# A two-layer graph network on one core: the leaky slope of the attention weights is split between ScalarE and VectorE

## The reference, cut to what matters

```python
scores = leaky_relu(e_s[edge_src] + e_d[edge_dst], 0.2)
m = segment_max(scores, edge_dst)
ex = exp(scores - m[edge_dst])
denom = segment_sum(ex, edge_dst)
msg = (ex / denom[edge_dst])[:, :, None] * h[edge_src]
agg = segment_sum(msg, edge_dst)
```

## Time and profile before

| | us |
|---|---|
| median of 3 runs | 2749.72 |
| lowest and highest of them | 2741.72, 2752.97 |
| the profiled execution, its own time | 2740.57 |
| span of its trace | 2738.8 |
| busy: PE, VectorE (DVE), GpSimd (POOL), ScalarE (ACT) | 1679.5, 1652.3, 1444.6, 833.9 |
| mean granted TensorE clock, share of full speed | 0.802 |

### The profile page before, as it was taken

The page is one execution under the profiler, slowest core; times in us unless marked ns, Lnnn a source line. Parts: engine busy times, 40 slices in busy tenths (PEclk is TensorE's granted clock), DMA queues, the critical chain, the costliest instruction groups (busy, mean ns, idle before and its releaser), DMA issues. The chain is left out here.

```text
span 2738.8 us, 38544 instructions
## 1 busy us (share of the span) xinstructions
PE 1679.5 (61%) x9983; PEld 1342.2 (49%) x9983; DVE 1652.3 (60%) x2687; ACT 833.9 (30%) x2134; POOL 1444.6 (53%) x1557
## 2 busy tenths in 40 slices
PE   4367534677655544486655777504477767767688
PEld 4255423455543433486544566403355545545577
DVE  6455763677654545676424655796366657668675
ACT  3144210000000000465212222205355545534454
POOL 3655676655656664526155555477665655530050
PEclk8599857788876776588777999856689888878899
DMA  4535544555423333344152545454555555331010
GB/s 137 183 101 159 178 140 123 170 174 157 120 81 92 95 92 106 112 142 131 51 175 81 163 154 160 161 190 128 157 166 170 172 164 158 106 101 32 4 43 31
DMA packets 132988, 346.47 MB, mean 127 GB/s; under 512 B 39881, under 2 KB 66521, under 8 KB 119347
## 3 DMA queue, kind: packets, MB, share of 16 engines
q0 software_dynamic: 66144, 180.94, 23.5%
q1 hardware_dynamic: 63407, 158.51, 16.5%
q10 hardware_dynamic: 3364, 6.16, 0.7%
HBM read 262.24 MB, written 83.28 MB: 126 GB/s over the span
## 5 line engine op out<-in xcount | busy, mean ns | idle before, releaser
L1366 PE MATMUL ms_ps_m<-ms_msg,ms_pick 128*128 128x260 f32 x1408 | 415.6, 458 | 287.1 <-issue 199.8
L892 POOL DMA_INDIRECT e_ring<-table,e_index x465 | 442.6, 952 | 252.2 <-issue 137.6
L1347 DVE TENSOR_TENSOR ms_msg<-e_ring,ms_ps_w 128x1040 f32<-128x1040 f32 (+1 forms) x352 | 436.6, 1240 | 141.8 <-issue 128.0
L1366 PEld LDWEIGHTS ms_ps_m<-ms_msg,ms_pick 128*128 128x128 f32 x1408 | 313.0, 229 | 389.7 <-issue 332.2
L1366 PE MATMUL ms_ps_m<-ms_msg,all_xn 128*128 128x272 f32 x1408 | 386.0, 437 | 191.5 <-issue 167.1
L892 POOL DMA_INDIRECT e_ring<-table,l_index x369 | 353.9, 959 | 227.3 <-issue 111.1
L1366 PEld LDWEIGHTS ms_ps_m<-ms_msg,all_xn 128*128 128x128 f32 x1408 | 290.0, 212 | 287.3 <-issue 218.9
L767 PE MATMUL sc_ps_e<-sc_keys,sc_hot 125*128 125x100 bf16 (+1 forms) x3840 | 322.7, 241 | 168.6 <-DVE all_xn L712 141.7
L767 PEld LDWEIGHTS sc_ps_e<-sc_keys,sc_hot 125*128 125x128 bf16 x3840 | 276.8, 104 | 238.8 <-issue 123.4
L934 POOL DMA_INDIRECT w_staged<-table,l_stage_index x256 | 257.3, 1005 | 183.5 <-issue 66.9
L670 ACT ACTIVATE sc_rows<-sc_ps_b 125x512 bf16<-125x512 f32 x320 | 171.2, 598 | 433.6 <-PE sc_ps_b L755 251.8
(11 more groups left out here) (513 smaller groups left out, 2743.3 us busy)
## 6 DMA issues: line engine op xcount, KB each, us to landing
ahead<-w_staged SPq DMA_DIRECT2D x32, 1056.0 KB
e_ring<-ahead SPq DMA_DIRECT2D x32, 1056.0 KB
ahead<-e_ring SPq DMA_DIRECT2D x20, 1040.0 KB
e_ring<-ahead SPq DMA_DIRECT2D x20, 1040.0 KB
e_ring<-table,e_index POOLq DMA_INDIRECT x465
all_acc<-ahead SPq DMA_DIRECT2D x27, 256.0 KB
ahead<-all_acc SPq DMA_DIRECT2D x27, 256.0 KB
e_ring<-table,l_index POOLq DMA_INDIRECT x369
```

The source lines that it names most:

```text
L892: pool.indirect_dma_start(out=g.ring[:, slot * QUAD + i // GT, i % GT, :], out_offset=None, in_=s.table[:, :], in_offset=bass.IndirectOffs ...
L1347: dve.tensor_tensor(msg[:, b, :, 0:R].rearrange("p t (h o) -> p t h o", h=H), ring[:, bass.ds(slot, 1), :, :].rearrange("p a t (h o) -> p ...
L1366: mm = pe.matmul(ps_m[b][:, 0:W], pick[:, b, t, :], msg[:, b, t, :], start=t == 0, stop=t == GT - 1)
```

## The change

Nothing is altered outside of `edge_weights`. The four PSUM banks `ps_t` become one tensor, of which two pairs of banks serve as two buffers of 640 columns, `lean`. For each line ScalarE writes 0.2 times the line into a `lean` buffer (function `slopes`), and VectorE takes the maximum of the line and the copy (`raise_line`). ScalarE writes copy i when all additions of the part have been made and VectorE has used copy i-2; VectorE waits for copy i on the new semaphore `leaned`. PE now waits, before it turns anything back, for the last maximum of the last part, since it writes into the same banks.

```diff
-        ps_t = [m.ps(f"ps_t{i}", [P, 4 * P]) for i in range(4)]
+        ps_all = m.ps("ps_t", [P, 4, 4 * P])
+        ps_t = [ps_all[:, i, :] for i in range(4)]
+        lean = ps_all.rearrange("p (a i) c -> p a (i c)", a=2)[:, :, 0:CL]
...
+        by_head, leaned = m.sem("by_head"), m.sem("leaned")
+        adds = GH * (2 if self_loops else 1)
+        lines_of = lambda part: [line[:, h, :] for line in (full, src_line) for h in range(part * GH, (part + 1) * GH)]
+        added = lambda part: H + part * (adds + 3 * GH) + adds
...
             pe.wait_ge(copied, banks)
+            pe.wait_ge(by_head, added(groups - 1) + 2 * GH)
...
+            def slopes(part):
+                for i, line in enumerate(lines_of(part)):
+                    act.wait_ge(by_head, added(part) + max(i - 1, 0))
+                    act.activation(lean[:, i % 2, :], line, ACT.Copy, scale=NEG).then_inc(leaned, 1)
+
+            for part in range(groups):
+                slopes(part)
+
             def exponentials(part):
...
-                for line in (full, src_line):
-                    add_each(heads, lambda h: dve.scalar_tensor_tensor(out=line[:, h, :], in0=line[:, h, :], scalar=NEG, in1=line[:, h, :], op0=ALU.mult, op1=ALU.max))
+                lines = lines_of(part)
+                for first in range(0, 2 * GH, GH):
+                    def raise_line(i):
+                        dve.wait_ge(leaned, part * 2 * GH + i + 1)
+                        return dve.tensor_tensor(lines[i], lines[i], lean[:, i % 2, :], ALU.max)
+                    add_each(range(first, first + GH), raise_line)
```

More of the change, by code:

```diff
@@ L1015, in edge_weights @@
         shifted, exp_ready, back_turned, back_copied = *(m.sem(n) for n in ("shifted", "exp_ready", "back_turned")), between.back_copied
-        by_head = m.sem("by_head")
+        by_head, leaned = m.sem("by_head"), m.sem("leaned")
+        adds = GH * (2 if self_loops else 1)
+        lines_of = lambda part: [line[:, h, :] for line in (full, src_line) for h in range(part * GH, (part + 1) * GH)]
+        added = lambda part: H + part * (adds + 3 * GH) + adds
         banks = H * CT // 4
@@ L1148, in _ @@
                     add_each(heads, lambda h: dve.scalar_tensor_tensor(out=full[:, h, :], in0=dst[:, h, :], scalar=2.0, in1=full[:, h, :], op0=ALU.mult, op1=ALU.max))
-                for line in (full, src_line):
-                    add_each(heads, lambda h: dve.scalar_tensor_tensor(out=line[:, h, :], in0=line[:, h, :], scalar=NEG, in1=line[:, h, :], op0=ALU.mult, op1=ALU.max))
+                assert heads_done[0] == added(part)
+                lines = lines_of(part)
[4 more added lines that the diff above has]
+                    add_each(range(first, first + GH), raise_line)
                 add_each(heads, lambda h: dve.tensor_tensor(src_line[:, h, :], src_line[:, h, :], full[:, h, :], ALU.subtract))
```

## The result

| | before | changed |
|---|---|---|
| median of 3 runs, us | 2749.72 | 2780.83 |
| lowest and highest, us | 2741.72, 2752.97 | 2763.69, 2799.22 |
| span of the profiled execution, us | 2738.8 | 2797.5 |
| ratio of the times, with its 95% interval | | 1.0115 [1.006, 1.0171] |

A forecast was written before the change was run, and what follows sets the result against it. VectorE was taken to bound the weights stages, but the message stage's start and POOL's restart to count. Delays of 0.5 (first layer) and 6.2 us (second) sum to +6.7, from median 2749.7 to 2756.5 us; range 2745 to 2773.

The forecast's parts named there:

- Price of the copy and of the maximum: Weights stages, per 640-column line: ScalarE's copy to PSUM 0.715 us, VectorE's maximum against PSUM 0.82 us.
- Price of a part: Weights stages: eight lines handed from ScalarE to VectorE cost each part 1.7 us more, 0.87 us a line against 0.745.
- Table load: ScalarE, after the last slope copy: 1.3 us in the second layer, hidden at no cost in the first.
- Order of ScalarE's work: Second layer: all exponentials and copies back follow the last slope copy, ending at 1893.9, so messages start 14.6 us late.
- ten copies 10.24: Second layer, ScalarE: part 0's ten copies back take 10.24 us, from 1871.4 to 1881.6.
- Ten more copies 10.0: Second layer, ScalarE: the ten copies back after part 1's exponentials take 10.0 us, from 1883.9 to 1893.9.
- those 9 us: Second message stage: 9 us between the second step's sum and POOL's restart, by which a start can be late unharmed.
- How much of the late start reaches the end: Message stages: 0.5 of 1.7 us in the first layer, 6.2 of 14.6 in the second; partial shift, chance 0.55.
- the whole late start comes through: Rival, both message stages: the full 1.7 + 14.6 = 16.3 us reaches the end, 2766 us; chance 0.27.
- the late start is hidden altogether: Rival, second message stage: gathers and their transfers pace it, so 0 to +2 us, 2751; chance 0.13.
- POOL runs freer: Rival, weights stages: gathers beside the maxima no longer slowed, 2.5 us gained, 2747 us if POOL bounds; chance 0.05.

The follow-up runs named there:

- free conditions: Conditions of the last five runs: the kernel before took 2317.16 us, then 2311.89, where it had taken 2739 to 2756 in the conditions of the result.
- the order alone: Kernel before, no slope copies, but both parts' exponentials behind the last subtraction: 2798.3 us, ratio 1.0129; in the free conditions 2309.79 us, 0.9989.
- banks of their own: Changed kernel with four other PSUM banks for slope copies, part 1's made after part 0's exponentials and ten copies back: 2777.83 us, ratio 1.0054.
- the pause: The order alone, with some 9 us of ScalarE idle time between the tenth copy back and the second exponentials: one run, 2774.65 us.
- the kernel with extra instructions: Kernel before, with 60 tiny memsets on VectorE behind the second layer's last subtraction: one run, 2731.22 us for 2739.31 of the kernel before.
- POOL was held: POOL waits before its third message-stage quad for all copies back: the order alone so held (second layer only) 2755.63 us, ratio 1.0055; changed kernel 2780.14, 1.0073.
- the changed kernel held: Changed kernel, with POOL waiting for all copies back before its third quad of message-stage gathers: 2780.14 us, ratio 1.0073.

## Why the prediction was wrong

**Price of the copy and of the maximum: right.** 0.707 us for the 0.715 of the sum, and 0.82 for 0.82.

**Price of a part: right in size.** 1.4 to 1.9 us for 1.7; a line took 0.83 us in a steady row for the 0.87 forecast.

**Table load: right.** 1.30 us in the second layer, hidden in the first, where it ran at 377.57 and the exponentials waited 2.65 us more for the subtractions. The Trainium skill ("ScalarE: Activation LUTs", What ACT_TABLE_LOAD costs) would have 2.66 us; no row here shows the drain of 1.38 that it adds.

**Order of ScalarE's work: right; its pace: wrong.** From the end of the last slope copy to the last copy back the prediction had 27.4 us (1866.5 to 1893.9). In the free conditions it is 27.3 (from 1519.1 to 1546.4). **In the conditions of the result it is 55.6** (from 1880.7 to 1936.3). This is the step that failed: "ten copies 10.24" was priced at the pace of the earlier trace rows, and these ten took 38.6 us, because TensorE's updates of `back_turned` came up to 28 us late and ScalarE waited for them. "Ten more copies 10.0" was right. In the first layer the five copies had gaps of 1.22 and 2.35 us in the same way, and its 1.7 us became 5.4.

The sign of it stood in the rows. The earlier trace rows have a hold that ends with "remote", 9 us after the sum that should have ended it, and the prediction booked those 9 us as slack that a late start could use up. They were a late update. Had it been read so, the same lateness could have been asked of the row of copies. Why the ten copies of part 0 ran without a gap before, beside gathers into the ring as well, was not found.

**How much of the late start reaches the end: not refuted.** The prediction let 8.4 of 14.6 us pass, because POOL's restart lay 9 us later than the sum that frees it. In the changed kernel it came 8.1 us after the first message (1949.58 to 1957.67) for 17.1 before, and 8.7 was forecast. Whether the end followed is less clear. The change's own profile has the message stage at 557.6 us for 556.2, so all of its late start came through; the order alone, banks of their own and the pause have 544.4, 548.9 and 551.6. But the kernel with extra instructions, which started the stage 4 us late, has 545.2, so this length scatters by as much as is asked for. The times do not settle it either: the change lost 31 us for 42.5 + 5.4 of late start, the order alone 35.5 by its ratio and 42.6 by the medians for 43.2. Where POOL was held, nearly all came through or more: 15 us for 18.0, and 20 for 14.5 in the changed kernel held. By the prediction's own steps with the 28.3 us put in, the sum is 6.7 + 28.3 = 35 us, or 2784.7, for 2780.8 measured.

**The rivals.** That the whole late start comes through gives 16.3 us and 2766 without the gaps, and 2794 with them; that lies above the median, though within the three runs. That the late start is hidden altogether is false for the result and true in the free conditions: with a first message that waits 29.6 us for its transfer, 11 us more of tail cost nothing. That POOL runs freer may hold there, and for more than its 2.5 us: 8 to 9 us between the medians (0.9962). The Trainium skill ("SBUF — State Buffer", Who interferes with whom) has that VectorE with two SBUF inputs contends with a GpSimd instruction that reads SBUF, and with one it does not. The trace agrees (up to 1.16 us for 0.95, and no long block beside the maxima against PSUM), but it also has a block that outlasts twelve VectorE instructions, which a lock for one instruction does not give. That the change's gain in the free conditions comes from the missing blocks is read from the profiles; the order alone, which keeps VectorE's slope, has 0.9989 [0.997, 1.0008] and no block in its profile. The change and the order alone have nearly the same median (2309.22 and 2309.79); what differs more is the kernel before in their two batches (2317.16 and 2311.89). So the timed runs do not settle it.

**What stays open.** What makes TensorE's updates and the other engines' register instructions late, and whether the two have one cause. The same kernel on the same chip took 2739 us in one batch of runs and 2317 in the next, eight minutes later, and 2312 on another chip. The late updates go with POOL's gathers (tail 23.8 us for 51.8 when held, 30.7 for 55.8), and a pause of ScalarE does not help. How much of the 427 us between the conditions they make was not tried. The Trainium skill ("Runtime: NRT & Kernel Launch", Instruction fetch mechanics) has that each sequencer refills its instructions by a DMA queue of its own and that this is mostly hidden. The trace agrees in so far as it lists such packets, none longer than 1.7 us in the changed kernel's first profile and none in its gaps, so late refills are not what opened them. Nor was it tried whether fewer gathers in this stretch, with the rest made up later, would help.

## What to carry to other kernels

Before work is moved, look at what the receiving engine already does between its pieces: here ScalarE's idle time beside VectorE was where part 0's exponentials and ten copies ran for free, and a split that put them behind the last line cost far more than the 0.08 us a line it changed. Do not price a long row of short, mutually waiting instructions at the pace of a short one, if the trace shows waits that end "remote" near indirect gathers: compare the time of the semaphore's update with the end of the work that it tells of. In a row that waits for TensorE at every step this lag grows with the row (0.4 us at the fourth copy, 28 at the tenth). And time a small change in more than one batch: this one is 1.2% slower or 0.4% faster by conditions that the program does not set.

## What the runs showed of the hardware

- While POOL issues indirect gathers, TensorE's semaphore updates can come late: 3 to 29 us after the transposes that they tell of, with gaps of 1.5 to 9.3 us between copies of 1.0 us. With POOL held at its third quad there is no gap (tail 23.8 us for 51.8). The sum of the earlier trace rows that ended at 1900.57 was reported at 1908.94.
- In the same profiles register instructions of VectorE, ScalarE and SyncE take up to 1.4 us, and memsets that wait for nothing have pauses of 0.6 us.
- Both belong to conditions that the program does not set: 83 of 122 updates beside gathers into the ring late in the first profile of the kernel before and none of 174 in its last, 550 register instructions over 0.4 us and none. On one chip its time was 2739 us in one batch and 2317 in the next. The durations of VectorE's groups are unchanged (1240 and 1241 ns, 426 and 424, 743 and 742).
- A gather beside a row of VectorE slope operations on SBUF takes up to 1.16 us for 0.95, and now and then it lies blocked to the row's end (9.7 us). Beside the operations with a PSUM operand neither was seen.
- A copy of 640 columns from SBUF to PSUM takes 0.707 us on ScalarE, and a maximum of an SBUF and a PSUM line of 640 takes 0.82 us on VectorE, 0.07 us more than the slope operation that it replaces takes in a row (0.745).
